# Another stage order for the second cross attention and the routing of a Flamingo block with two mixtures of experts

## The reference, cut to what matters

```
q = heads(layernorm(x) @ Wq.T);  k, v = heads(ctx @ Wk.T), heads(ctx @ Wv.T)   # 16 heads of 8
w = softmax(where(mask, q k^T / sqrt(8), -1e9))
x = x + tanh(g_xattn[1]) * ((w v) @ Wo.T)
n = layernorm(x)  normed again, * gamma + beta
probs = softmax(n @ router_w.T);  two largest of 8, gates = softmax(their probs)
x = x + tanh(g_ffn[1]) * (sum over the two experts of gate * swiglu_e(n) + swiglu_shared(n))
```

## Time and profile before

| | |
|---|---|
| three runs, median | 369.37 us (368.71 to 370.1) |
| profiled execution, its time and span | 368.7 us, 368.7 us (368.71 is one of the three runs) |
| busy: TensorE, VectorE, ScalarE, GpSimd | 274.0, 251.1, 213.6, 151.1 us |
| first scores product of the stretch | 146.87 us |
| last slot numbers | 232.91 us |
| first product of the expert loop | 251.55 us |

### The profile page before, as it was taken

One profiled execution on the slowest core, in us unless ns is written; L12 is line 12 of the kernel. 1 busy time (PEld: TensorE's weight loads), 2 busy tenths in 40 slices (PEclk: granted clock), 3 DMA queues, 4 the chain that ended last, 5 costly groups with the idle time before them and its releaser, 6 DMA issues.

```text
span 368.7 us, 7937 instructions
## 1 busy us (share of the span) xinstructions
PE 274.0 (74%) x2143; PEld 202.4 (55%) x2144; DVE 251.1 (68%) x884; ACT 213.6 (58%) x503; POOL 151.1 (41%) x201
## 2 busy tenths in 40 slices
PE   3499880395899876899897862536999999999810
PEld 2398780153677554577575751223776676776510
DVE  3256259996577631778889966833988788887475
ACT  1555549775577595845763534301877777777430
POOL 2412358960222510811732677760344444444502
PEclk9999996589899968999898855655999999999975
DMA  7860000620000000000000011221222122221173
GB/s 187 272 260 0 3 0 9 221 93 0 3 1 2 1 2 0 3 0 2 0 3 7 32 52 44 88 75 44 53 59 63 54 58 58 58 58 36 46 239 103
DMA packets 19469, 21.06 MB, mean 57 GB/s; under 512 B 3184, under 2 KB 17008, under 8 KB 18800
## 3 DMA queue, kind: packets, MB, share of 16 engines
q1 hardware_dynamic: 16992, 15.79, 14.1%
q0 software_dynamic: 2304, 4.77, 4.0%
q10 hardware_dynamic: 144, 0.15, 0.2%
HBM read 14.28 MB, written 6.42 MB: 56 GB/s over the span
## 4 chain that ended last, share of the span: by engine, by line
PE 54%; DVE 18%; issue 7%; POOL 7%; DMA 5%; ACT 5%; SPq 2%; DVEq 0%; POOLq 0%; ACTq 0%
PE bank L1160 43%; POOL dispatched_rows L787 5%; PE bank L1482 3%; DVE x L1151 2%; DMA region_q<-expert_rows 2%; DMA wr<-in 2%; DVE region_k L883 2%; PE bank L1462 2%; DVE region_k L967 2%; DVE top L882 2%; DVE nm L965 1%; ACT x_hat L514 1%; PE bank L1213 1%; PE bank L1196 1%; DVE bn_raw L838 1%
## 5 line engine op out<-in xcount | busy, mean ns | idle before, releaser
L814 POOL DMA_INDIRECT expert_rows<-region_k,slot_dest x40 | 38.2, 955 | 63.3 <-DVE slot_dest L1110 62.4
L1160 PE MATMUL bank<-w_high,slot_rows_t 128*128 x160 | 47.2, 337 | 3.2 <-issue 1.9
L681 ACT ACTIVATE region_w<-bank 128x384 f32<-128x384 f32 x40 | 19.6, 490 | 35.6 <-PE bank L1160 34.8
L787 POOL DMA_INDIRECT dispatched_rows<-region_t,slot x32 | 31.9, 997 | 16.1 <-issue 9.2
L1160 PE MATMUL bank<-w_high,region_x 128*128 (+1 forms) x272 | 35.8, 228 | 2.3 <-DVE region_t L908 2.1
L1128 DVE SCALAR_TENSOR_TENSOR region_w<-bank,region_w 128x384 f32<-128x384 f32 x40 | 22.3, 557 | 16.4 <-ACT region_w L681 15.3
L686 ACT ACTIVATE region_x<-bank 128x768 f16<-128x768 f16 x40 | 32.2, 804 | 0.9 <-PE bank L1482 0.9
L729 POOL TENSOR_SCALAR minus_mean_rstd<-mean_var 128x4 f32<-128x4 f32 x16 | 3.4, 213 | 71.1 <-DVE mean_var L841 45.7
L740 POOL TENSOR_TENSOR w_low<-w_scaled,w_high 128x512 f16<-128x512 f32 (+1 forms) x23 | 29.0, 1286 | 0.0
L514 ACT ACTIVATE x_hat<-x,minus_mean_rstd,rstd 128x128 f32<-128x128 f32 x64 | 26.2, 482 | 4.4 <-POOL minus_mean_rstd L732 4.4
L1160 PE MATMUL bank<-w_low,region_x 128*128 (+1 forms) x136 | 27.1, 227 | 0.0
(11 more groups left out here) (238 smaller groups left out, 785.0 us busy)
## 6 DMA issues: line engine op xcount, KB each, us to landing
w_scaled<-in SPq DMA_DIRECT2D x5, 1024.0 KB, 8.2
slot_rows<-dispatched_rows SPq DMA_DIRECT2D x40, 65.5 KB, 1.9
region_q<-expert_rows SPq DMA_DIRECT2D x4, 512.0 KB, 5.7
x<-in SPq DMA_DIRECT2D x4, 256.0 KB, 4.4
region_w<-in SPq DMA_DIRECT2D x2, 512.0 KB, 6.9
out<-x SPq DMA_DIRECT2D x4, 256.0 KB, 2.6
w_scaled<-in SPq DMA_DIRECT2D x1, 704.0 KB, 4.0
expert_rows<-region_k,slot_dest POOLq DMA_INDIRECT x40, 2.2
```

The lines of the kernel that those rows point to most:

```text
L681: act.activation(sil[:, v, :], bank[2 * v][:, 0:FF], ACT.Silu, scale=1.0 / WS).then_inc(silu_done, 1)
L787: pool.indirect_dma_start(disp, bass.IndirectOffsetOnAxis(slot[:, b * T + t, c:c + 1].bitcast(U32), 0), pay[:, b * T + t, :], None).then_i ...
L814: pool.indirect_dma_start(ytok, bass.IndirectOffsetOnAxis(dst[:, r:r + 1].bitcast(U32), 0), yv[:, r, :], None).then_inc(rows_sent[r], 16)
L1160: return pe.matmul(o, l, r, start=start, stop=stop)
```

## The change

Only the numbers in the tables of the four engines differ. No instruction is added or taken away. In the order of the tiles the stages of one tile come closer together: shift to add was 4.4 tiles, now 2.6. keys_out moves ahead of the weight chunks on ScalarE, the weight splits on POOL are spread in another way between the rstd of the batches, and send and send2 move relative to rstd2.

```
-C_PE = {"scatter": -5.2, "keys": -5.1, "xt": 0.5, "scores": 1.6, "et": 3, "pv": 4, "ot": 5.5, "w": 6, "turn": 9.1,
-        "logits": 10.5, "rank": 11.4}
+C_PE = {"scatter": -5.2, "keys": -5.1, "xt": 0, "scores": 1, "et": 2.1, "pv": 2.6, "ot": 3.2, "w": 3.6, "turn": 5.6,
+        "logits": 6.2, "rank": 7.1}
...
-C_POOL = {"rstd": -9.7, "low": -5.3, "rstd2": -4.2, "send": 1.8, "send2": 5.4}
+C_POOL = {"rstd": -4.6, "low": -4.85, "rstd2": 4.2, "send": 7.5, "send2": 8.4}
```

More of the change, by code:

```diff
@@ L71 @@
 C_EVERY = 1
-C_PE = {"scatter": -5.2, "keys": -5.1, "xt": 0.5, "scores": 1.6, "et": 3, "pv": 4, "ot": 5.5, "w": 6, "turn": 9.1,
-        "logits": 10.5, "rank": 11.4}
[L74 to L77, removed]
-C_POOL = {"rstd": -9.7, "low": -5.3, "rstd2": -4.2, "send": 1.8, "send2": 5.4}
+C_PE = {"scatter": -5.2, "keys": -5.1, "xt": 0, "scores": 1, "et": 2.1, "pv": 2.6, "ot": 3.2, "w": 3.6, "turn": 5.6,
+        "logits": 6.2, "rank": 7.1}
+C_ACT = {"chunk": -4.9, "norm": -0.3, "keys_out": -5, "xt_out": 0.4, "exp": 1.7, "e1t": 2.3, "ont": 3.4, "norm2": 4.4,
+         "high": 4.9, "turn_out": 5.9, "exp_logits": 6.6}
+C_DVE = {"residual": -4.8, "shift": 1.3, "over_sum": 2.9, "add": 3.9, "affine": 4.6, "low": 5.2,
+         "shift_logits": 6.4, "route": 6.8, "slots": 7.4}
+C_POOL = {"rstd": -4.6, "low": -4.85, "rstd2": 4.2, "send": 7.5, "send2": 8.4}
 C_ID, C_HM, C_HR, C_S, C_S128, C_EREG, C_I8, C_P8, C_2T = 0, 128, 144, 160, 208, 256, 264, 272, 280
```

## The result

The changed kernel takes 398.52 us in the median of four runs (393.18 to 402.92), beside 369.74 us (368.71 to 371.25) of the kernel before: 1.064 times as long, with a 95% interval of 1.055 to 1.073. The forecast was 392.7 us in a range of 380 to 403.

The account below looks back on a forecast made before the run. The stretch from first scores to last slots was taken as bounding, with TensorE's work setting clean steps. Start 149.0, steps 81.2 and drain 13.0 give 243.2; the tail puts experts 23.3 us later: 392.7 us, range 380 to 403.

Parts of the forecast that it names:

- the hold: Four GpSimd sends delay the next batch's rstd2 by 5.3 us from slots; steps 10 and 14 take 11.0 us, +14.5.
- rival 2: Statistics come late enough that the sends stay covered; each of three holds loses about 4.1 us: 379 us, chance 0.09.
- The clean step: A tile step without batch work grows from 2.84 to 3.7 us, because w waits for ScalarE's copy; 15 steps 55.6.
- e1t: ScalarE's 0.59 us operation after TensorE's et in each tile step; the copy that w waits for comes behind it.
- the norms in the copies' way: ScalarE normalisations of 1.64 us in steps 3 and 6 stand ahead of copies TensorE waits for: +2.9 us.
- The 15 steps: First to last tile: clean steps, batch work, holds and low clock sum to 81.2 us, against 56.8 before.
- The low clock: TensorE runs at 1.2 GHz in the step after the first hold: +1.7 us.
- the two steps with a scatter: Scatter 2 and 3, 1.95 us each in TensorE's queue, one partly covered: +3.4 us.
- Rival 3: TensorE at 1.2 GHz in four to six steps, +2.7 us each, or sends slowed by VectorE: 402 to 410, chance 0.09.
- The start: Early keys_out on ScalarE waits for the keys, so first scores come near 149.0, 2.2 us later than 146.87.
- The drain: From scores of tile 15 to the last statistics 13.0 us, putting these at 243.2.
- The tail: Last rstd2 held until 247.4, last slots 260.6; experts start 14.3 us after slots instead of 18.6, at 274.9.

Follow-up runs that it names:

- the two experiments on the hold: Changed kernel with rstd2 ahead of the previous batch's sends: 381.07 us, ratio 1.026; kernel before with send2 moved ahead of rstd2: 375.87 us, ratio 1.013.
- The filler in two of the places: Changed kernel plus 24 unread 128x384 products ahead of w of tiles 8 and 12: 392.14 us, ratio 1.055.
- The late-keys trace: Changed kernel with ScalarE's keys_out back behind five weight chunks and the norm: 396.15 us, ratio 1.059; with rstd2 also ahead of the sends: 381.04 us, 1.025.
- the kernel with covered hops: Changed kernel with rstd2 ahead of the sends and pv, ot, w and all behind them moved later: 397.46 us, ratio 1.059.
- fillers: Kernel before plus unread products: 8 ahead of the last batch's turn, 8 ahead of its rank, 24 ahead of the expert loop: 371.53 us, ratio 0.999.

## Why the prediction was right, point by point

**The mechanism and the sign hold.** Three holds of rstd2 behind four sends were named as the largest term, and the two experiments on the hold show it. Going by the ratios it is worth 14 us (give or take 4); rival 2, the case without it, was put at 379, and the kernel without it measured 381.

**The hold's parts.** From slots to rstd2 I took 5.3 us: it measured 5.4, 5.1 and 5.1 (slots ready at 194.65, 220.82 and 242.96; L729 at 200.04, 225.92 and 248.04). Past its statistics rstd2 was held 4.4, 4.1 and 3.1 us, where 4.1 was put three times. Steps of 11.0 each: 11.58 and 11.28. TensorE idle "some 7 us": 5.85 and 6.93 ahead of w.

**The clean step** was 3.7 and measured 3.78, with the idle 0.75 us where it was foretold. Its size is right. That the term can be taken out on its own, which the sum might suggest, is not: w waits for ont, behind it pv for e1t, then scores for xt_out, then the batch stages for theirs. No experiment turned the shorter clean step into a shorter kernel, so how much of the 10 us that stay without the hold is the hops' own isn't settled. The rows name three candidates: 3.78 instead of 2.84 in each clean step, the norms in the copies' way, and the clock.

**The 15 steps were 4 us too small**: 81.2 against 85.27. The low clock, which I charged with 1.7 us in the one step behind the first hold, was mis-sized. Rows show it in six tiles' scores, 0.89 us more for each pair of products. In both holds w and v_blocks ran at it too: from w to the next mask product it is 2.16 and 2.15 us (203.79 to 205.95, 229.66 to 231.81), where the sum had 1.04, together 2.2 us. The filler in two of the places makes three steps 3.0 us shorter in its trace and points to 3.5 us in the times. Another part stands in the two steps with a scatter, 6.60 and 5.57 us (150.48 to 157.08, 169.66 to 175.23), 1.4 more than 2 x 3.7 + 3.4; the first of them began at the low clock. How much of the 4 us is the clock's in all wasn't measured. Rival 3 had this mechanism with some 9 us and more; it came at under half of that.

**The start** was put at 149.0 for the first scores, 2.2 us late, and they came at 146.56. From the first scatter product it is 16.34 us instead of 15.77 (131.10 to 146.87), 0.6 more. What I had missed is that the keys, with the banks free, run in one piece; what I had not seen at all is what follows from the move: TensorE stands idle for 6.34 us ahead of xt and then does the first tiles at 1.2 GHz. The late-keys trace has 3.2 us less by the seventh tile, but the times with and without late keys (1.059 and 1.064, 1.025 and 1.026) show no such cost. So the landmark was wrong, and whether the move costs anything near 2.2 us isn't shown.

**The drain** was 13.0 from scores(15) and measured 13.1 (231.81 to 244.90).

**The tail.** Last statistics 244.9 (forecast 243.2); from rstd2's end to the last slots 11.2 (11.3); last send 9.4 us after the slots (9.3); experts 15.2 after them instead of 14.3, since the last send's landing and load took 5.8 and not 5.0 (270.46 to 276.27). The 3.4 us given back against 18.64 stand in the trace, but they were not to be had alone: the kernel before with earlier sends paid for them in holds.

**The base.** I took the profiled execution's time for its span, since 368.71 was one of the runs. Where both are on record a run takes 1.8 to 1.9 us more than its span (395.8 and 394.0; 393.27 and 391.4; in the kernel before 370.55 and 368.7), so that execution was more likely one of about 370.5 us (an estimate), above the median and not under it. The forecast doesn't change by it: it is the median 369.4 plus the 23.3 us of the sum either way. Like for like, the span was to be 392.0 and was 394.0.

**What was luck.** These 2.0 us are less than the errors in them: start -2.4, steps +4.1, drain +0.1, last statistics to last slots -1.2 (16.16 against 17.4), from there to the experts +0.9, the rest +0.6. That they nearly cancel is luck; the mechanism and the largest terms are not.

**The rule weighed.** The Trainium skill (SBUF — State Buffer, the two separate sides) has a DMA from GpSimd's queue, of some 620 ns alone, take some 3100 ns beside a VectorE copy, because its descriptors wait for the shared port. As an estimate from that page four sends would have held rstd2 for about 12 us; it was 5.1 to 5.4. In the first hold VectorE was busy for 2.50 of 5 us (195 to 200), with reductions, statistics and elementwise operations and no copy, and the sends took 0.96 to 1.22 us. So no send was slowed that much, but these runs don't test the rule for copies.

## What to carry to other kernels

When stages of an in-order pipeline are pulled closer together, look in each queue at what stands between a short operation on the path and the one ahead of it: the four sends held nothing up while their slots came 7 us before the statistics (200.50 and 207.39), and held rstd2 3.1 to 4.4 us past its statistics once the two came within 2 us. A distance in the order that seems to be slack can be cover, and for a stage of several hops cover for all of them at once: here restoring a single hop showed the next. The last stretch can gain by such a move (3.4 us here) while the steps ahead lose more (28.5), so price both.

## What the runs showed of the hardware that was not expected

TensorE stayed at 1.2 GHz over 30 us in the profiled execution of the kernel with covered hops, though it was busy for 85 to 90% of each 10 us (195 to 225 us, above). That was the longest of its four runs, and why the clock stayed low isn't shown. In the kernel before, fillers that raised the granted clock of the last stretch from 0.54 to 0.70 changed the time by nothing that could be measured (0.995 to 1.002).
